# Order of the steps in a routed expert MLP: two groups of transposes side by side, then two products

## What is computed

```
router_logits = x_flat @ w_router                     # 2048 tokens, 8 experts
top_vals, top_idx = top_k(router_logits, 2)
probs = softmax(top_vals)
h = square(relu(x_flat @ w_fc[e]))                    # 512 -> 512, per expert
y = h @ w_proj[e]                                     # 512 -> 512
out = sum over the two chosen experts of y * prob
```

## Time and profile before

| | |
|---|---|
| median of 3 runs | 1469.9 us (1468.97 to 1472.49) |
| the profiled execution's own time | 1471.34 us |
| its span | 1469.7 us |
| PE busy | 1425.4 us (97%) |
| DVE, ACT, POOL busy | 772.0, 727.4, 414.4 us |
| slot steps 3 to 36 | 219.6 us |

### The profile page before, as it was taken

One profiled execution on the slowest core, in us unless ns is written; L12 is line 12 of the kernel. 1 busy time (PEld: TensorE's weight loads), 2 busy tenths in 40 slices (PEclk: granted clock), 3 DMA queues, 4 the chain that ended last, 5 costly groups with the idle time before them and its releaser, 6 DMA issues. The chain is left out here.

```text
span 1469.7 us, 26490 instructions
## 1 busy us (share of the span) xinstructions
PE 1425.4 (97%) x7946; PEld 1204.1 (82%) x7947; DVE 772.0 (53%) x1813; ACT 727.4 (49%) x1633; POOL 414.4 (28%) x409
## 2 busy tenths in 40 slices
PE   7999999999999999999999999989999989999994
PEld 5888888888888888888888888878888877888883
DVE  6555655555555655555565565545555563333334
ACT  5565655655656555556565565622222223333334
POOL 1222121212122212122122121103233445335475
PEclk9999999999999999999999999999999999999998
DMA  5242333232323333223323335433348445675699
GB/s 179 75 128 93 107 97 124 86 114 85 115 93 107 109 113 102 98 92 108 103 97 126 95 107 177 145 112 137 130 124 215 133 173 208 244 263 194 209 205 236
DMA packets 86547, 200.45 MB, mean 136 GB/s; under 512 B 15856, under 2 KB 16496, under 8 KB 83184
## 3 DMA queue, kind: packets, MB, share of 16 engines
q1 hardware_dynamic: 75728, 149.66, 31.5%
q0 software_dynamic: 10784, 50.36, 12.2%
HBM read 160.05 MB, written 92.62 MB: 172 GB/s over the span
## 5 line engine op out<-in xcount | busy, mean ns | idle before, releaser
L375 POOL TENSOR_TENSOR small<-small,half 128x4 f32<-128x4 f32 x193 | 194.7, 1009 | 770.0 <-DVE small L404 770.0
L503 DVE CUSTOM_DVE_ANT_0 logit<-score_ps,bias 128x128 f32<-128x128 f32 (+3 forms) x256 | 124.8, 488 | 156.7 <-PE score_ps L629 117.7
L309 ACT ACTIVATE prob<-logit,small 128x128 f32<-128x128 f32 (+3 forms) x256 | 144.2, 563 | 119.1 <-DVE small L503 115.3
L642 PEld LDWEIGHTS y_ps<-vs,prob_t 128*128 128x128 f32 x1280 | 175.0, 191 | 20.4 <-issue 3.7
L642 PE MATMUL y_ps<-vs,prob_t 128*128 (+1 forms) x1280 | 184.8, 275 | 0.3 <-DVE x_now L408 0.3
L316 ACT ACTIVATE prob_t<-prob_ps 128x128 f32<-128x128 f32 (+3 forms) x256 | 111.5, 436 | 54.5 <-PE prob_ps L635 53.4
L870 ACT ACTIVATE yt_hi<-turn_ps,subln 128x512 fp32r<-128x512 f32 x60 | 41.0, 688 | 154.8 <-PE turn_ps L1164 154.8
L635 PE MATMUL prob_ps<-ident,prob 128*128 128x128 f32 x640 | 112.6, 274 | 2.4 <-ACT prob L309 2.2
L568 PE MATMUL k_ps<-w_hi,x_hi 128*128 (+1 forms) x256 | 103.8, 405 | 6.4 <-DVE w_lo L443 6.4
L568 PE MATMUL v_ps<-w_hi,x_hi 128*128 (+1 forms) x256 | 106.5, 416 | 0.0
L568 PE MATMUL v_ps<-w_hi,x_lo 128*128 (+1 forms) x256 | 106.3, 415 | 0.0
(11 more groups left out here) (245 smaller groups left out, 3406.8 us busy)
## 6 DMA issues: line engine op xcount, KB each, us to landing
slots_x<-in_zeros SPq DMA_DIRECT2D x64, 512.0 KB, 5.4
y_scratch<-x_now SPq DMA_DIRECT2D x65, 256.0 KB, 3.0
x_raw<-in_x_t SPq DMA_DIRECT2D x64, 256.0 KB, 2.9
slots_y<-in_zeros SPq DMA_DIRECT2D x64, 256.0 KB, 5.2
y_raw<-y_scratch SPq DMA_DIRECT2D x14, 1024.0 KB, 5.9
w_raw<-in_w_experts POOLq DMA_DIRECT2D x7, 2048.0 KB, 8.3
w_hi<-in_w_experts POOLq DMA_DIRECT2D x7, 2048.0 KB, 13.3
w_raw<-in_w_all SPq DMA_DIRECT2D x16, 768.0 KB, 6.5
```

The costliest lines, as they stand in the source:

```text
L309: nc.scalar.activation(prob[:, 0:width], logit[:, 0:width], ACT.Exp, scale=-1.0, bias=least[:, h:h + 1], accum_out=row_sum[:, (i % 2) * HG ...
L375: nc.gpsimd.tensor_tensor(r, ms, half[:, :], ALU.pow).then_inc(ready, 1)
L503: nc.vector.tensor_tensor_reduce(out=logit[:, 0:width], in0=score_ps[:, 0:width], in1=bias[:, h, T - width:T], scale=1.0, scalar=3e38, op0 ...
L642: mm = nc.tensor.matmul(y_ps[:, h * D:(h + 1) * D], prob_t[:, j * P:(j + 1) * P], one(vs[:, bass.ds(now, 1), j, h * D:(h + 1) * D]), start ...
```

## The change

The order of work within a slot step is changed on three engines. PE turns the next but one tile's rows directly behind the squared rows of this tile, ahead of `up`, except in step 2 (`HEAD`), where the old order is kept. ACT and DVE handle the turned rows ahead of the relu and the square, in all steps, the second step too. SP and POOL are not edited.

```diff
 def slot_step(k, b, h, y, q):          # ACT
     round_hid(b, k)
+    if more(k, 2):
+        round_x(b, k + 3)
     if more(k, 1):
         rectify(1 - b, k + 1)
-    if more(k, 2):
-        round_x(b, k + 3)
     scale_out(k, b, y, q)

 def slot_step(k, b, h, y, q):          # DVE
     split_hid(b, k)
+    if more(k, 2):
+        split_x(b, k + 3)
     if more(k, 1):
         square(1 - b, k + 2)
-    if more(k, 2):
-        split_x(b, k + 3)

 def slot_step(k, b, h, y, q):          # PE
     turn_hid(b, k)
+    late = isinstance(k, int) and k == HEAD
+    if more(k, 2) and not late:
+        turn_x(b, h * 16 + 32)
     if more(k, 1):
         up(1 - b, load_owner(k + 1), k + 2)
-    if more(k, 2):
+    if late:
         turn_x(b, h * 16 + 32)
     down(b, load_owner(k), k)
```

## The result

| | before | after |
|---|---|---|
| median of 17 runs | 1471.68 us | 1480.87 us |
| the profiled execution, its span | 1471.34, 1469.7 us | 1479.22, 1477.5 us |
| start of `turn_hid(2)` | 1214.58 | 1211.31 |
| start of `turn_hid(3)` | 1221.63 | 1220.01 |
| start of `turn_hid(37)` | 1441.36 | 1449.28 |

The ratio is 1.0054, with a 95% interval of 1.0040 to 1.0069: the change costs 7.9 us (5.9 to 10.2). The runs of the changed kernel lie in two groups, six from 1473.5 to 1476.2 and eleven from 1479.2 to 1484.5, so its median lies in the upper one, and the medians differ by 9.2; the kernel before has 15 of its 17 between 1468.9 and 1474.4. One of its executions, at 1582.56 us, counts as slow and isn't in the ratio.

A forecast was written before the change was run, and what follows sets the result against it. PE's work was taken to bound the slot steps, 6.46 us each without waits. Terms 0 + 0 + 0 + 5.2 us, the last for late row loads, gave 1475.1 us against the median, 0.35% slower; range 1469.2 to 1478.6.

The forecast's parts named there:

- walk through the bursts: Row loads followed through POOL's six weight bursts: PE waits 0.8, 0, 0, 1.4, 1.5, 1.5 us, 5.2 in all.
- the sum corrects itself: PE's summed delay at the bursts: whatever burst 1 costs, 0.1 or 1.5, it is 2.2 us behind burst 4.
- Transposes next to transposes, product next to product: PE's slot steps: pairing like work saves or costs nothing, 0 taken; bounds 0.3 us and 0.7 us in all.
- The hidden rows' way: Relu, square, round and split between PE's pieces: still in time, cost 0; room of the longest square 0.92 us becomes 0.48.
- Loads in a burst take what is left to its end: Row loads issued 3.5 us or more behind a burst's start: issue plus landing is 14.9 us, the burst's end.
- The cap of 11.5 us: Row loads issued between 2 and 3.5 us behind a burst's start: each taken to need 11.5 us to land.
- The bursts keep their times: POOL's weight bursts: times unchanged, since each starts when POOL has landed and split the one before.
- "None" at bursts 2 and 3: Row loads at bursts 2 and 3: issued 5.95 and 4.9 us in, taking 9.0 and 10.0 us, no PE wait.
- The read of the owner register is hidden: PE's register read between products: hidden by the products in the queue, 0 taken, at worst 0.7 us.
- the loads landing in time: Rival: row loads land in time despite the bursts and nothing changes, 1469.9 or 1472.5 us; chance 0.34.
- a gain from the pair: Rival: paired transposes save a change of kind in PE's slot steps, at 0.2 a step 6.8 us, 1463.1; chance 0.04.
- The third: Rival: longer waits, the square's shorter room or late gates on SP make bursts dearer, 8.4 us, 1478.3; chance 0.07.

The follow-up runs named there:

- four_parts_after: The changed kernel with four buffers of gathered rows instead of two, so each row load has about 23 us instead of 10; ratio to the kernel before 0.9988.
- table_all: The changed kernel with SP's table reads put ahead of its wait for the output rows in every step; ratio to the kernel before 1.0044.
- after_third: The changed kernel run a third time without further edit, for a third trace; 1483.76 us, its 34 slot steps 231.38 us.
- nine_splits: The changed kernel with nine instead of eight subtractions on POOL for each turn of weights; ratio to the kernel before 1.0098, with five runs.
- owner_first: The changed kernel with PE's read of the next tile's owner register put ahead of the wait for gathered rows; ratio to the kernel before 1.0052.
- seven_splits: The changed kernel with seven instead of eight subtractions on POOL for each turn of weights; ratio to the kernel before 1.0048.
- pe_alone: The kernel with PE in the changed order, ACT and DVE left in the order of before; ratio to the kernel before 1.0052.
- after_again: The changed kernel run again without further edit: the second, clean trace, no half clock in the slot steps; 1478.7 us, its 34 slot steps 228.12 us.

## Why the prediction was right or wrong

The direction, the place and the mechanism came out as forecast; the size didn't. The median was 1480.87 us against 1475.1, above the range's end of 1478.6. 1.8 us of that is the kernel before, whose median over 17 runs was 1471.68 instead of 1469.9. The change cost 7.9 us by the ratio, 9.2 by the medians, 8.2 at the bursts of the clean trace, against 5.2.

**The step that failed** is the walk through the bursts, the only term of the sum that isn't 0: 0.8, 0, 0, 1.4, 1.5, 1.5 forecast; 1.56, 1.07, 1.26, 1.24, 1.26, 1.82 measured in the clean trace. Since the sum corrects itself, what counts is how late the last late load lands, counted from `turn_hid(3)`: forecast 153.9 us (1375.72 less 1221.79), measured 156.7 (1375.63 less 1218.90), 2.8 later. Burst 6 itself came 1.6 later than I had it, and its load landed 15.5 behind the burst's start, not 14.3. The register's read behind the wait adds 0.65, once. The 0.25 that I took off the room, for which I had no row, wasn't there (the last late load landed at 1375.63, its transposes began at 1375.64), and the 23 steps up to it were 0.01 us longer each, which isn't part of the 8.2; these two take 0.4 back. Together 3.0, the difference between 8.2 and 5.2.

- **Transposes next to transposes, product next to product: right**, 0 taken and 0.01 us a step lost. **The hidden rows' way: right**; PE waited for the square in no slot step from 3 on of the changed kernel (in step 2 it did for 1.48 us, before for 1.50), and `four_parts_after` leaves nothing for ACT and DVE.
- **The load goes out at 3.07: nearly right**, 2.7 to 3.3 into most steps. **Loads in a burst take what is left to its end: right** for those issued 3.5 us or more behind its start, and shown twice, by 10.9 us for 3.9 us behind burst 3's start (14.8 together) and by `table_all`. **The cap of 11.5 us for those issued at 2 to 3.5: too low**; such loads took 12.1 at 3.36 (first trace), 12.0 at 3.26 (`after_third`) and 12.0 to 12.4 at 2.7 to 2.8 (`nine_splits`).
- **"The bursts keep their times": wrong.** Counted from `turn_hid(3)`, bursts 2 to 6 stood at 31.1, 59.8, 86.9, 114.1 and 141.2 us in the second trace, where they had stood at 30.4, 57.3, 84.5, 112.1 and 139.8 before: up to 2.6 later, since the first three bursts followed each other more slowly (29.15 and 28.67 us apart, 28.39 and 26.88 before). The first burst moved by chance: in the first trace POOL issued it 0.14 us ahead of `turn_hid(3)` instead of 1.99 behind it; 1.65 of these 2.13 us are step 2 at half clock. In the second trace it stood at 1.99 as assumed; the step was 1.56 us too long where I had 0.8: the load took 11.1 us, nearer to the upper of the two rows that I had averaged, and the register's read was on top.
- **"None" at bursts 2 and 3: wrong**, 1.07 and 1.26 in the clean trace. Burst 2's load took 10.3 us at 6.2 behind the burst's start, 16.5 together, where I had used the 14.9 of before. The burst itself was longer: 16.0 us from POOL's issue to its first subtraction, against 14.2 in the trace of before (1252.01 to 1266.19). It was 15.7 and 16.3 in the other two traces of the changed kernel. Why is open.
- **The read of the owner register is hidden: wrong behind a wait.** I called it hidden by the products in the queue in both pieces. That holds while PE runs, and not at a late load: 0.65 us there. In the sum it counts once, since the next late load is then later by as much less; that is why its removal (`owner_first`) showed no gain.
- **"The sum corrects itself": right, and not followed far enough.** I saw that the delay before burst 4 ended at 2.2 us whatever burst 1 did. The rule behind it is that the loss per burst is the spacing of the landings less four steps, 0.8 to 1.8 us from burst 3 on in the three traces. It then doesn't matter how the loss is made up, by a wait for rows or by a read. My 1.4, 1.5 and 1.5 for bursts 4 to 6 sum to 4.4, the clean trace's 1.24, 1.26 and 1.82 to 4.3; what was missing was bursts 2 and 3.
- **Slow clock: not forecast.** I left the clock out because PE never slowed in these steps before. 1.6 us behind burst 1 in two of three traces of the changed kernel.
- **"Each us that PE loses comes out at the end": so in the first trace**, with 28.2 us of span behind `turn_hid(37)` against 28.3 before. In the other two it was 30.0, and the chain there goes through POOL's gathers. No run here says whether the change has a part in that.
- The bound of 7.5 us for the sum assumed that only the room could be off; the bursts' times and the cap were, too. The range's end of 1478.6 would have held the 8.4 us of the clean trace's steps on a kernel before of 1469.9. That the median lies above it takes the 1.8 us of the kernel before and the upper of the two groups as well.

The rivals: the loads landing in time is refuted by the waits, a gain from the pair by the chain. The third, each burst costing 1.4 us, 8.4 in all, had 0.07 and came nearest in its number only: what it named, the room of the square and late gates, held PE nowhere.

## What to carry to other kernels

A buffer's room is the time from when its owner really issues the next load to when it is needed: moving a consumer earlier moves both only if the issuing queue was waiting for nothing else. Compare the room with the slowest load in a burst of another queue, not with the median. Where two periodic streams meet, as PE's steps and POOL's bursts here, a late load can lock them, and then the loss is the difference of their periods: what helped here was more buffers or no burst, and neither a quicker restart nor a load issued a little earlier into the burst.

## What the runs showed of the hardware

- A load of 256 KB on SP's queue took 2.6 us alone, and 8.6 (`seven_splits`) to 14.1 us (`nine_splits`) when issued into the first 6 us of 4 MB on POOL's. Issued 0.6 us earlier into burst 3 (`table_all`), it took 0.8 longer.
- A register read on PE cost 0.65 us where PE's queue had just been held by a late load, even where PE itself hardly stood still, and nothing in quiet steps, where the queue was full. The trace put 0.36 of it down to POOL's subtraction at most bursts, and moving the read took it away.
- PE's granted clock fell from 1.00 to 0.50 behind waits of 1.4 to 3.6 us in some places (1.80 in the first trace, 1.42 in `seven_splits`, 1.39 in `nine_splits`, 3.56 in `pe_alone`), and stayed at 1.00 behind waits of 0.72 (`after_again`), 1.44 (`owner_first`) and 1.75 (`nine_splits`). What decides isn't settled here.
